# Holding back side tasks beside diagonal pairs of attention steps, and a reciprocal moved behind the second maximum

## What is computed

```python
latent_kv = x @ w_kv_down          # rank 128
kv = latent_kv @ w_kv_up           # keys and values of 16 heads
q = x @ w_q
att = einsum('bqhd,bkhd->bhqk', q, k) * 64 ** -0.5
att = softmax(where(causal, att, -inf))
x = x + einsum('bhqk,bkhd->bqhd', att, v).reshape(...) @ w_out
```

## Time and profile before

| what | us |
|---|---|
| runs | 2165.53, 2170.82, 2171.48 |
| median | 2170.82 |
| profiled execution, device time | 2168.69 |
| its span, first to last instruction | 2167.3 |

### The profile page before, as it was taken

How to read it: one execution, slowest core, us unless ns; L and a number is a source line. 1 busy time by engine, 2 the same in 40 slices (tenths; PEclk the granted TensorE clock), 3 DMA queues, 4 the chain that set the end, 5 groups by cost and what they waited for, 6 DMA issues and landing times.

```text
span 2167.3 us, 35663 instructions
## 1 busy us (share of the span) xinstructions
PE 2013.0 (93%) x13104; PEld 1264.6 (58%) x13104; DVE 1340.9 (62%) x2711; ACT 1101.0 (51%) x2226; POOL 1426.3 (66%) x812
## 2 busy tenths in 40 slices
PE   5998578999999999999998999999999999999899
PEld 3666445556565656565655565656565665565466
DVE  5888646576656565656565656576656565656453
ACT  4776534445444444444464444445454444444575
POOL 0333214778787878787867687878787878687822
PEclk9999789999999999999999999999999999999999
DMA  3000000000000000000000000000000000000001
GB/s 114 1 1 1 8 8 6 11 19 11 19 11 19 11 19 11 19 11 19 11 19 11 18 11 18 11 19 11 18 11 18 11 19 11 18 11 11 25 25 59
DMA packets 25787, 37.03 MB, mean 17 GB/s; under 512 B 6544, under 2 KB 14864, under 8 KB 25616
## 3 DMA queue, kind: packets, MB, share of 16 engines
q1 hardware_dynamic: 25616, 34.76, 5.0%
HBM read 30.02 MB, written 4.46 MB: 16 GB/s over the span
## 4 chain that ended last, share of the span: by engine, by line
PE 71%; DVE 16%; ACT 5%; POOL 3%; issue 3%; DMA 0%; ACTq 0%; DVEq 0%; POOLq 0%; SPq 0%
PE heads_out L833 20%; PE beside L652 11%; PE two_heads L790 8%; PE scores L652 7%; PE scores L813 5%; PE scores L819 5%; PE scores L817 5%; PE scores L815 5%; DVE part_max L1021 3%; POOL acc L1319 2%; PE beside L844 2%; DVE stats L872 2%; PE beside L798 2%; PE two_heads L652 2%; ACT prob L1234 2%
## 5 line engine op out<-in xcount | busy, mean ns | idle before, releaser
L1319 POOL TENSOR_TENSOR acc<-acc,prob 128x1024 f32<-128x1024 f32 (+3 forms) x512 | 1017.5, 1987 | 195.3 <-ACT prob L1234 138.7
L1234 ACT ACTIVATE prob<-scores 128x512 f32<-128x512 f32 (+3 forms) x1280 | 579.4, 539 | 649.3 <-DVE scores L1031 327.4
L1021 DVE TENSOR_REDUCE part_max<-two_heads 128x2 f32<-128x1024 f32 x384 | 468.8, 1221 | 315.6 <-PE two_heads L790 315.3
L833 PE MATMUL heads_out<-prob,V 128*64 128x512 f32 (+3 forms) x2560 | 544.9, 547 | 0.0
L1018 DVE CUSTOM_DVE_ANT_0 two_heads<-two_heads,mask 128x128 f32<-128x128 f32 (+3 forms) x512 | 242.0, 514 | 188.4 <-PE two_heads L790 188.3
L790 PE MATMUL two_heads<-k_hi,q_hi 64*128 64x512 f32 (+3 forms) x1280 | 273.8, 423 | 56.9 <-DVE part_max L1021 27.1
L833 PEld LDWEIGHTS heads_out<-prob,V 128*64 128x64 f32 x2560 | 156.9, 137 | 225.3 <-issue 203.2
L790 PEld LDWEIGHTS two_heads<-k_hi,q_hi 64*128 64x128 f32 x1280 | 120.5, 184 | 249.2 <-issue 143.0
L813 PE MATMUL scores<-q_hi,k_hi 64*128 64x512 f32 (+3 forms) x1280 | 235.9, 364 | 1.2 <-ACT neg_max L1221 0.8
L819 PE MATMUL scores<-neg_max,sel 64*128 64x512 f32 (+3 forms) x1280 | 235.4, 362 | 0.0
L817 PE MATMUL scores<-q_lo,k_hi 64*128 64x512 f32 (+3 forms) x1280 | 235.4, 362 | 0.0
(11 more groups left out here) (294 smaller groups left out, 3077.0 us busy)
## 6 DMA issues: line engine op xcount, KB each, us to landing
rden<-rden_rows SPq DMA_DIRECT2D x128, 128.0 KB, 2.9
wP_raw<-wPair SPq DMA_DIRECT2D x16, 384.0 KB, 3.1
X<-u SPq DMA_DIRECT2D x8, 512.0 KB, 8.9
out<-X SPq DMA_DIRECT2D x8, 512.0 KB, 2.9
den<-den_rows SPq DMA_DIRECT2D x64, 4.0 KB
rden_rows<-inverse SPq DMA_DIRECT2D x64, 4.0 KB, 1.3
wA_sb<-wA SPq DMA_DIRECT2D x1, 768.0 KB, 7.0
wFa<-wF SPq DMA_DIRECT2D x1, 768.0 KB, 7.8
```

The lines of the kernel that those rows point to most:

```text
L833: made = pe.matmul(heads_out[head(h), x0:], V[(idx - j + c) % NVS][:, tt, head(h)], prob[step % NPROB][:, h, x0:], start=t == 0, stop=t == ...
L1021: made = ve.reduce_max(part_max[:, t, :, c:c + 1], two_heads[:, :, 0:width], AX.X)
L1234: ac.activation(prob[step % NPROB][:, h, x0:], bank(task, h)[:, x0:], ACT.Exp).then_inc(empty(task, h)[0], 1)
L1319: po.tensor_tensor(total[:, :, x0:], total[:, :, x0:], new[:, :, x0:], ALU.add).then_inc(acc_ok, 1)
```

## The change

It does three things in the planner. In a diagonal place a filler may only be a `value` or a `turn_max`, or one that is due within two steps. The halves of `project` are due three steps later than before. `invert` stands behind the scores and the second maximum of its place instead of before the scores. No instruction is added or removed.

```diff
-        def filler(latest):
+        def filler(latest, diagonal):
+
+
             open_ = sorted((x for x in fillers if x[0] <= s and x[2] not in self.done), key=lambda x: x[1])
+            if diagonal:
+                open_ = [x for x in open_ if x[2][0] in ("value", "turn_max") or x[1] <= s + 2]
             if open_ and open_[0][1] <= latest:
                 fillers.remove(open_[0])
                 self.need(*open_[0][2])
...
             if kind == "two_parts":
-                fillers.extend([(s + 2, s + 4 + half, ("project", ready[0][1][1], half)) for half in range(2)])
+                fillers.extend([(s + 2, s + 7 + half, ("project", ready[0][1][1], half)) for half in range(2)])
...
             if self.at < goal:
                 maximum()
-            due("invert")
             for step in steps[s:s + 2]:
                 self.need("score", *step)
             if self.at < goal:
                 maximum()
             else:
                 chore()
+            due("invert")
             if s == 0:
                 self.add("first_layers_done")
-            filler(10 ** 6)
             diagonal = not steps[s:s + 2] or any(t >= TPB * UNITS[idx][2] for idx, t in steps[s:s + 2])
+            filler(10 ** 6, diagonal)
             if not diagonal:
                 self.side_bank = 0
-                filler(s + 8)
+                filler(s + 8, False)
                 self.side_bank = 7
...
             if not due("denominators") and diagonal:
-                filler(s + 8)
+                filler(s + 8, True)
...
             for _ in range(4):
-                filler(10 ** 6)
+                filler(10 ** 6, False)
```

## The result

| | before | after |
|---|---|---|
| median of the runs | 2171.15 (2165.53 to 2172.63, 4 runs) | 2198.82 (2195.80 to 2206.22, 4 runs) |
| profiled execution | 2168.69 | 2197.48 |
| its span | 2167.3 | 2196.1 |

The account below looks back on a forecast made before the run. TensorE bounds the kernel, busy 104.27 of 106.93 us per regular pair, so only its waits count. 13.0 + 4.2 + 2.6 + 6.0 - 2.0 = 23.8 us on 2168.69 gave 2192; 8-in-10 range 2170 to 2208.

Parts of the forecast that it names:

- Which tasks move: The two projections of unit j=2, refused in places 36 and 38, go to places 0 and 2 of the next pair.
- Boundary: Places 36 and 38 and the next pair's 0 and 2: +0.87 us each, times 15 = +13.0.
- Place 36: Diagonal place that loses two projections: 1.82 us saved, 0.91 for each.
- place 38: The second projection's addition to X no longer stands in front of the first reduction: 0.15 us saved.
- place 2: Gains a projection, 0.91; first maximum reduced behind the query's `q_lo`, +0.72, read from a like case with a key; sum +1.63.
- place 0: Next pair's first place gains a projection, 0.91, and the query waits about 0.3 behind it: +1.2 us.
- the wait for the addition to X: In place 0 the query waits until VectorE has added the projection to X: about 0.3 us, bounds 0 and 0.69.
- Reordered fillers: Later due places reorder fillers: place 24 waits 0.3 in 14 pairs, +4.2; place 12 waits 0.2 in 13, +2.6.
- Reciprocal, place 6: The reciprocal comes directly in front of `k_lo` on VectorE, making it 0.46 us later: +6.0 in 13 pairs.
- Reciprocal, place 10: With the reciprocal no longer between the two reductions, the next first maximum waits less: -0.14 us, -2.0 in 14 pairs.
- Late `scale_out`: GpSimd's `scale_out` starts up to 3 us later, hidden by GpSimd's idle time: 0, at most 1 us per pair.
- Irregular pair: First sequence's last pair, also carrying `turn_tiles` and `latent` for the second: 0, bounds -6 and +8 us.

Follow-up runs that it names:

- the filter alone: Kernel before with only the diagonal-place rule, projections due as before and reciprocal as before: 2172.93, ratio 1.0020.
- the best version: Kernel before, subtraction behind fillers, place 10's reciprocal behind the second maximum, place 22's filler between maxima; last, fillers from 8 and 36 to 10 and 38: 2134.66 (0.9849).

## Why the prediction was right, step by step

The prediction was 2192 in a range of 2170 to 2208; the median is 2198.82. Direction and mechanism held. Point by point:

- **Which tasks move.** The order came out as derived: places 36 and 38 without a filler, projection, `weigh` and query in place 0, projection in place 2.
- **Boundary, +0.87 forecast, +0.80 measured.** Place 36 -1.82 and -1.81; place 38 -0.15 and -0.16; place 2 +1.63 and +1.67; place 0 +1.21 and +1.10. The one difference is the wait for the addition to X: 0.19 us instead of 0.3. The price of place 2 came from a row with a *key*, and the query costs the same. The version with the query first and the late slot in another bank shows cause, not only size.
- **Reordered fillers, +6.8 forecast, +10.6 measured** (14 x 0.44 + 13 x 0.34; the run with the due places alone gave +10.2). Both waits were close, 0.34 for 0.3 and 0.23 for 0.2. The step that was mis-sized is "so I take a wait of 0.3" and its "0.2" at place 12, taken as the whole price: the first product behind it took 0.11 us longer, its weight load too coming only with it, and that stands in no wait.
- **Reciprocal, place 6, +0.46 forecast, +0.40 measured.** That an earlier start of the subtraction wins nothing is shown from both sides, by the changed kernel (starts earlier, ends alike) and by the version with the reciprocal ahead (starts later, ends alike). By the page "SBUF — State Buffer" of the Trainium skill, section "SBUF: two separate sides", the lock holds for a whole instruction. The traces agree that the end doesn't depend on the start, with 0.28 and 0.29 us from the sum's end to the subtraction's in all four kernels. A block until the sum's end would leave the subtraction's whole 0.41 us behind it, and there the traces show less.
- **Reciprocal, place 10, -0.14 forecast, -0.14 measured.** In the times of whole runs the reciprocal's two terms (+3.2 together) can't be confirmed: removed from the changed kernel it is worth 1 us, added to the kernel before it is 3 in the profiled execution and about 10 by the ratio. What the clock does in single places is as large.
- **Late `scale_out`, 0 forecast.** Its wait for the transfers rose by 111.7 us, the one for ScalarE fell by 82.5, and ScalarE's exponentials waited less for GpSimd. GpSimd's idle time was the cover, as said.
- **Irregular pair, 0 forecast, +0.5 measured.** Right in size here, but fragile: with the filter alone it was 9.3 longer in the slowest of ten executions, more than the upper bound of 8.

With measured places the terms give 15 x 0.80 + 10.6 + 5.2 - 2.0 = 25.8 against 28.8 in the span. The forecast sum, 23.8, had no term for the clock and none for the last pair's end. In this pair of executions the clock took 1.5 us in place 2 of pair 1 (below) and gave back 3.2 in pair 0, and the last place 36 with the tail took 1.3. That leaves about 3.5 us, which I did not settle. So that the sum comes within 5 us of the span is partly luck: what the clock does differs by as much between executions of like work.

## What to carry to other kernels

A side task is never just its products: it holds a bank until the last engine has read it, and it takes a turn in the queue of that engine. Place it where TensorE waits for something else, between two operations that share a buffer, rather than where it seems to be in nobody's way. Filling such gaps brought 13 us in the last step and was the main part of the 1.5% of the best version, which also moved the subtraction and the reciprocal. The change of this document cost 1.4% in all; the rule for the diagonal places by itself cost next to nothing (ratio 1.0020), and 12 of the 28 us came of the two tasks that it and the later due places together sent over the boundary. When an operation is moved past another on a queue, ask who stands behind its new position. When a wait is made, add that the weight load behind it is held back too (0.11 us here).

## What the runs showed of the hardware

**The subtraction ends with the other engine's sum.** With two inputs in SBUF it takes 0.41 us where GpSimd runs no sum (at 336.61 in the kernel before). Beside the sum it ends 0.28 or 0.29 behind the sum's end, whether it began 1.34, 1.15, 0.89 or 0.36 us ahead of that. The rest after the block is less than the 0.41 alone, so it isn't begun anew; how the block is shared out inside was not measured.

**The clock falls in a place with a long wait.** TensorE has the same work in each place 2. One of the changed kernel's is above (775.10, 4.86 us busy, clock 1.00). Here are another of it, in pair 1, and one of the version with the reciprocal in its old place, in pair 13:

```profile
445.36:453.51 8.15, 6.39 (x44) 3.54 (x44) 5.64 (x17) 1.60 (x5) 2.95 (x4) 0.79 0.01 2
...
1773.50:1781.17 7.67, 6.44 (x44) 3.44 (x44) 4.51 (x13) 1.60 (x5) 2.94 (x4) 0.78 0.00 0
```

TensorE's longest waits in them, from its timeline:

```profile
448.32 0.60 PE L794 MATMUL two_heads<-k_hi,q_hi 64*128 64x512 f32 x2 [1.76 <-DVE part_max L1022]
...
1775.92 0.49 PE L794 MATMUL two_heads<-k_hi,q_hi 64*128 64x512 f32 x2 [1.23 <-DVE part_max L1022]
```

After 1.76 and 1.23 us without work the granted clock averaged 0.79 and 0.78 over the place, so part of it ran at the lower of the two levels, 1.2 GHz instead of 2.4. The second lasts 7.67 us for what takes 6.09 at full clock, with the same wait: 1.58 us lost, more than the wait. In the first VectorE has four instructions more (statistics of a layer norm, L876 and L878), two of them ahead of the reduction. These make the wait 0.54 longer, and the other 1.53 of its 8.15 us are TensorE's busy time, 6.39 instead of 4.86. A place at the second sequence's start also fell, to 0.83, behind a wait of 1.75.

The length of the wait alone doesn't decide it. Waits of 1.22 and 1.23 us at the other boundaries left the clock at 1.00, and so did one of 1.83 in the irregular pair of the version with the filter alone. Which places fall differs between executions too: with the same fillers, place 2 of pair 0 had 0.83 in the kernel before and 1.00 with the reciprocal moved. What decides it was not found. So a wait can cost its own length again or more, and two executions can differ by some us without a difference in the plan. In the irregular pair with the filter alone TensorE is busy for 122.49 us with 798 instructions, for which the kernel before needs 117.57: 5 of the 9.3 us are work at a lower clock.
